# Cross-attention with a quantised feed-forward: the row maxima of the scores made in tiles of 64 rows by 32 columns

## The reference, cut to what matters

```python
xn = layer_norm(layernorm(x), g1, b1)           # x: 8 x 1024 x 512
cn = layer_norm(context, g2, b2)                # context: 8 x 2048 x 512
q, k, v = xn @ Wq.T, cn @ Wk.T, cn @ Wv.T       # 16 heads of 32
scores = einsum('bqhs,bkhs->bhqk', q, k) / sqrt(32)
attn = softmax(scores, axis=-1)                 # over 2048 keys
x = x + einsum('bhqk,bkhs->bqhs', attn, v).reshape(...) @ Wo.T + bo
x = x + mx_quantised(layernorm(x)) @ mx_quantised(weight).T + bias   # blocks of 32, fp6 grid
```

## Time and profile before

| | |
|---|---|
| median of 3 runs | 4500.66 us (4495.67 to 4505.8) |
| profiled execution | 4507.71 us |
| its span | 4505.9 us |
| granted TensorE clock, mean | 0.993 |
| PE busy | 96% |
| DVE, ACT, POOL busy | 76%, 62%, 60% |

### The profile page before, as it was taken

The page is one execution under the profiler, slowest core; times in us unless marked ns, Lnnn a source line. Parts: engine busy times, 40 slices in busy tenths (PEclk is TensorE's granted clock), DMA queues, the critical chain, the costliest instruction groups (busy, mean ns, idle before and its releaser), DMA issues.

```text
span 4505.9 us, 89640 instructions
## 1 busy us (share of the span) xinstructions
PE 4345.9 (96%) x36880; PEld 1506.5 (33%) x36880; DVE 3443.6 (76%) x4023; ACT 2814.4 (62%) x5128; POOL 2718.9 (60%) x1706
## 2 busy tenths in 40 slices
PE   4999999999999999999999999999999999999999
PEld 2322343223432234322343223422234222342223
DVE  5788667886678866888668886688866888668885
ACT  3387734877447864478645785458754587546784
POOL 2288552885428854388544885348853588525884
PEclk9999999999999999999999999999999999999999
DMA  5355642557326573356633556335663365543654
GB/s 191 73 118 118 150 136 61 120 118 180 109 59 123 114 192 99 68 117 121 177 100 69 119 120 175 102 77 116 123 167 106 75 123 115 167 111 74 123 113 108
DMA packets 190012, 532.35 MB, mean 118 GB/s; under 512 B 28625, under 2 KB 102673, under 8 KB 148386
## 3 DMA queue, kind: packets, MB, share of 16 engines
q0 software_dynamic: 43776, 318.79, 35.3%
q1 hardware_dynamic: 145826, 207.83, 15.0%
HBM read 110.98 MB, written 21.01 MB: 29 GB/s over the span
## 4 chain that ended last, share of the span: by engine, by line
PE 73%; DVE 12%; DMA 5%; ACT 4%; issue 3%; POOL 2%; SPq 0%; DVEq 0%; ACTq 0%; POOLq 0%
PE banks L1048 20%; PE banks L1060 17%; PE banks L956 16%; PE banks L1016 12%; PE banks L1091 5%; DVE max_parts L621 5%; DMA wdT<-wkT_wvT_wqT 3%; ACT region L835 2%; PE banks L925 2%; DMA sums<-wkT_wvT_wqT 2%; PE banks L950 1%; DVE amax L569 1%; DVE x_stats L536 1%; DVE region L759 1%; DVE qscale L571 1%
## 5 line engine op out<-in xcount | busy, mean ns | idle before, releaser
L621 DVE TENSOR_REDUCE max_parts<-banks 128x2 f32<-128x1024 f32 x2048 | 2402.1, 1218 | 454.3 <-PE banks L1016 442.4
L835 ACT ACTIVATE region<-banks 128x512 f32<-128x512 f32 x4096 | 2191.1, 616 | 506.2 <-PE banks L1048 401.1
L427 POOL TENSOR_TENSOR wkT_wvT_wqT<-region 128x1024 f32<-128x1024 f32 x528 | 1284.7, 2518 | 668.0 <-ACT region L835 662.6
L1048 PE MATMUL banks<-queries_stacked,keys_stacked 98*32 98x512 f16 x16384 | 1317.7, 384 | 21.6 <-ACT values L822 7.1
L1060 PE MATMUL banks<-region,values 128*32 128x512 f32 x8192 | 1076.8, 600 | 12.3 <-ACT region L835 9.2
L1048 PEld LDWEIGHTS banks<-queries_stacked,keys_stacked 98*32 98x32 f16 x16384 | 415.5, 95 | 1149.3 <-ACT region L835 842.0
L1016 PE MATMUL banks<-keys_stacked,queries_stacked 33*128 33x512 f16 x4096 | 701.5, 386 | 7.2 <-DVE max_parts L621 3.5
L956 PE MATMUL banks<-region,wkT_wvT_wqT 128*128 128x512 f16 x2304 | 557.3, 381 | 12.6 <-DMA wkT_wvT_wqT<-weights_split 10.3
L427 POOL TENSOR_TENSOR sums<-region 128x1024 f32<-128x1024 f32 x144 | 358.8, 2617 | 92.1 <-ACT region L835 91.8
L956 PE MATMUL banks<-wkT_wvT_wqT,region 128*128 128x512 f16 x1536 | 368.8, 380 | 0.0
L1016 PEld LDWEIGHTS banks<-keys_stacked,queries_stacked 33*128 33x128 f16 x4096 | 180.2, 93 | 559.4 <-issue 352.2
(11 more groups left out here) (92 smaller groups left out, 3224.0 us busy)
## 6 DMA issues: line engine op xcount, KB each, us to landing
wdT<-wkT_wvT_wqT POOLq DMA_DIRECT2D x96, 1024.0 KB, 11.7
wkT_wvT_wqT<-wkT_wvT_wqT POOLq DMA_DIRECT2D x80, 1024.0 KB, 7.3
sums<-wkT_wvT_wqT POOLq DMA_DIRECT2D x72, 1024.0 KB, 7.3
wkT_wvT_wqT<-sums POOLq DMA_DIRECT2D x40, 1024.0 KB, 7.2
region<-in_x SPq DMA_DIRECT2D x24, 1024.0 KB, 8.9
wkT_wvT_wqT<-weights_split SPq DMA_DIRECT2D x8, 3072.0 KB, 19.0
keys_stacked<-region SPq DMA_DIRECT2D x384, 64.0 KB, 2.0
keys_stacked<-sums SPq DMA_DIRECT2D x384, 64.0 KB, 2.0
```

The costliest lines, as they stand in the source:

```text
L427: e.tensor_tensor(SUMS[dst][:, half], PR[i][:, half], PR[i + 1][:, half], ALU.add).then_inc(s_pr, 1)
L621: e.tensor_reduce(mpart[:, buf, :, a, t, c], MXB[parity], AX.X, ALU.max).then_inc(s_mxd, 1)
L835: e.activation(PR[u % 4][:, j * HALF:j * HALF + HALF], score_bank(m % NU, kt, j)[0], ACT.Exp, scale=SCALE).then_inc(s_ex, 1)
L1048: mm = e.matmul(dst[HD * t:HD * t + HD, :], KA[0:STR, ds(ka + (j * C + (u + 1) * P + HD * t), HD)], QA[0:STR, ds(qa[j], HALF)], start=True ...
```

## The change

In the steps, `max_part` now calls `max_pair` with a width of 32 (HD). The 128 columns of each of the two matmuls are made as four matmuls of 32 columns, each with its own weight load, the two heads taking turns: eight matmuls of 64 rows by 32 columns in place of two of 64 rows by 128 columns. They read the same rows, stream the same 512 keys and write the same PSUM addresses; the semaphore is raised by the last of the eight. The front still calls it with 128 columns. No other engine's instructions change.

```diff
-                def max_pair(parity, g, q, r, h):
+
+                def max_pair(parity, g, q, r, h, width=P):
                     a, t, c = piece(r, h)
-                    for i in range(2):
-                        rows = ds(2 * HD * i, HD + 1)
-                        mm = e.matmul(MXB[parity][:, i, :],
-                                      QA[rows, ds(((2 * g + q) * J + 2 * a + i) * HALF + t * P, P)],
-                                      KA[rows, ds((g * J + 2 * a + i) * C + c * HALF, HALF)], start=True, stop=True)
+                    for w in range(0, P, width):
+                        for i in range(2):
+                            rows = ds(2 * HD * i, HD + 1)
+                            mm = e.matmul(MXB[parity][w:w + width, i, :],
+                                          QA[rows, ds(((2 * g + q) * J + 2 * a + i) * HALF + t * P + w, width)],
+                                          KA[rows, ds((g * J + 2 * a + i) * C + c * HALF, HALF)],
+                                          start=True, stop=True)
                     mm.then_inc(s_mxf, 1)
...
                     def max_part(h):
                         e.wait_ge(s_mxd, count + (h + 1))
-                        max_pair(h, *piece_of, h)
+                        max_pair(h, *piece_of, h, HD)
```

## The result

| | before | changed |
|---|---|---|
| median of 7 runs each | 4506.67 us | 4522.51 us |
| profiled execution | 4507.71 us | 4522.12 us |
| its span | 4505.9 us | 4520.3 us |
| TensorE instructions with a record (PE, and as many PEld) | 36880 | 46864 |

The ratio is 1.0042, with a 95% interval of 1.0032 to 1.0052: the change makes the kernel slower by 0.42%, 19 us (14 to 23). (The ratio goes by the means, which differ by 18.5 us; the medians in the table differ by 15.8.) The forecast was 4511 against the 4500.66 shown then, +10 us. The measured time is inside the range and on the forecast side, but the cost is nearly twice the forecast one.

A forecast was written before the change was run, and what follows sets the result against it. TensorE, 96% busy, was taken as the bound, with VectorE or exponentials delaying some steps. Passages and instructions added 0, and 468 steps at 0.021 us added 10 us: 4500.7 to 4511 us, range 4437 to 4545.

The forecast's parts named there:

- The passages cost what they did: TensorE going into and out of maxima: each change of tile shape still costs about 0.1 us, so this term is 0.
- The eight tiles overlap: Each round of maxima: eight tiles run at once, with the last delayed by some 3 ns a tile.
- The supply of instructions is no limit: A step's 40 matmuls and 40 weight loads cost 0; at 36 ns an instruction they would add 0.3 us.
- The last tile starts about 20 ns later: End of each maxima round: eight tiles delay the last start by 18 to 42 ns, taken as about 20.
- the steps with sums: 4 of 16 steps, where sums follow the maxima: the 20 ns count fully, in 208 steps.
- The handing over to VectorE: Semaphore after a pair of maxima: VectorE starts later by as much as the last tile, about 20 ns.
- the prediction's own loop: VectorE's two reductions a step: period plus distance from first to second pair is about 2.85 us.
- the steps bound by VectorE: 5 of 16 steps, where the second pair waits for VectorE: the 20 ns count once, in 260 steps.
- Nothing in the steps that wait for exponentials: 7 of 16 steps, held up behind the maxima: 0.1 to 0.2 us of waiting takes in the 20 ns.
- The halving in VectorE's loop: Steps where VectorE bounds: a saving elsewhere in TensorE's step is halved, as the second pair waits longer by the other half.
- That the passages come free: Rival at the maxima's shape changes: equal column counts pass free, 0.17 us less a step, −55 us, 4446 us; 22%.
- That tiles or instructions come one after the other: Rival in the maxima rounds: tiles in two groups, 260 us more, 4760 us, or slow instruction supply, 250; 14%.

The follow-up runs named there:

- run 5: Run 4 with 98 rows in place of 33, so maxima have the scores' tile shape, 128 by 32: 4458.64 us, ratio 0.9892 against the kernel before.
- run 4: Changed kernel, each call in the steps making only its first head (four matmuls of 33 rows by 32 columns): 4503.17 us, ratio 0.9995 against the kernel before.
- run 7: Changed kernel with VectorE reducing only the first 256 of 512 keys of each head: 4495.66 us, ratio 0.9975 against the kernel before.
- run 6: Kernel before with VectorE reducing only the first 256 of 512 keys of each head: 4488.69 us, ratio 0.9961 against the kernel before.
- the clearing matmul: Kernel before with each 32-row by 128-column matmul of zeros made as four of 128 rows by 32 columns: 4488.96 us, ratio 0.9954.
- Half the split: Changed kernel with width 64 in the steps, four matmuls of 64 by 64 a pair: 4515.87 us, ratio 1.0014 against the kernel before.

## Why the prediction was right, and where its sizes were off

*The passages cost what they did: right, and shown.* The prediction read it off three passages, none of them the one in question. The timeline after shows 0.57 from maxima to sums. Taken from the last start of one kind to the first start of the next, where nothing waits, scores to maxima is 309 ns before and 307 after, and maxima to what follows 305 to 308 in both; in run 5, where the shapes are equal, the same two are 204 and 207. Runs 4 and 5 show the passage of rows alone at 32 columns and what its absence is worth. The Trainium skill ("TensorEngine Tiling (Array Packing)", Key Properties) states that a change of the tiling mode drains TensorE. The traces agree in so far as every pair of unlike tile shapes that follow each other without a wait has these 0.1 us more; that it is a drain they don't show.

*The eight tiles overlap: right.* An M entry grew by 0.02 us, and its two rounds still start 225 ns apart. *The supply of instructions is no limit: right.* The step from 1526.67 to 1529.21 in the changed timeline takes 2.54 us with 80 instructions, 32 ns each, below the 36 that the earlier trace rows had shown as possible, and the steps that wait for exponentials have the same period with 80 instructions as with 56.

*The last tile starts about 20 ns later: right in size, 23 ns after the first against 3.* That it counts in full in the steps with sums is right (run 7 against run 6).

*The handing over to VectorE: the step that was mis-sized.* "It counts at the end of M [...] and at the semaphore, so that VectorE starts later by as much": it starts later by 50 ns, not 20. Put into the prediction's own loop, period plus distance of the pairs is 2.90 in place of 2.85 and PE's rest is 20 ns longer, so the period grows by (50 + 20) / 2 = 35 ns; the table has 197 ns over the six steps that VectorE bounds, 33 a step. Where a step with sums also waits for VectorE (step 2), it pays both, 62. So the terms are 48 × 0.197 = 9.5 us for the steps bound by VectorE, where the prediction had 260 × 0.021 = 5.5, and 7.0 us for the 192 steps with sums, where it had 208 × 0.021 = 4.4. The prediction counted too many steps of both kinds (it took all 52 units for alike), which made its sum too high by under a tenth; the hand-over that it took as 20 ns made it too low by much more. The two terms make up the 16.4 us that the step periods give, a little under the measured 19, whose interval holds it.

*Nothing in the steps that wait for exponentials: right.* Six of the seven differ by 1 ns at most; the seventh (step 7), which waited for VectorE as well, paid 12. The halving in VectorE's loop fits too (35 ns worked out, 33 measured), though the prediction took one of two alternating periods (2.54, the other is 2.47) for the period of this kind.

*The rivals.* That the passages come free is excluded by the timeline and by run 5. Its sum of −55 us for 0.17 us less was near the −44.5 that run 5 has against run 4, but in part by luck: three of the steps with sums gained 0.23 to 0.24 us where the sum had 0.17, and the steps that VectorE bounds 0.02 to 0.07 where it had 0.08, since they meet the next bound. That tiles or instructions come one after the other is excluded by the M entries.

## What to carry to other kernels

Write down the tile shape (rows by columns) of every matmul in a chain that keeps TensorE full, and count the places where it changes: each cost 0.1 us here, whether rows, columns or both changed, and a small matmul of an odd shape between others pays it twice. Making one dimension alike bought nothing here; only the whole shape did, as run 5 (−44.5 us for the rows alone, with the columns already alike) and the clearing matmul (−0.46%) show. Splitting a matmul into more tiles without reaching the neighbour's shape only delayed its last tile and its hand-over. Before counting what a saved stall is worth, sort the steps by what they wait for behind it: here 6 of 16 took in the whole cost.

## What the runs showed that was not expected

- A pair made as eight tiles reached VectorE 50 ns later than as two (482 against 432 ns from its first matmul), of which the later last start is 20. Four tiles of 64 by 64 took 462; four of one head, 64 by 32, 449; four of one head, 128 by 32, 441. The Trainium skill ("TensorE: Matmul & The Clock Gate", The cost: per-tile semaphore tail) gives 4.7 ns a tile for the tail behind the last matmul, from which an estimate for six more tiles is 28 ns. The runs have 31 for eight against two (459 and 428 from the last start), but 24 for two more tiles of 64 columns; the count of tiles alone does not explain that.
- The order of the eight tiles (heads in turn, or one after the other) changed neither this nor the time.
- Two rounds of four tiles of 64 by 64 start 240 ns apart, where two rounds of two tiles of 64 by 128, or of eight of 64 by 32, start 225 apart. Half the split therefore cost TensorE as much as the whole one; why is open.
- Halving VectorE's work in the reductions brought 0.4%, although VectorE bounded a third of the steps: the next bound, the exponentials, lay only 18 ns a step below (steps 10 to 13).
